# Splitting the turned scores around the key projection in a six-layer local-attention kernel

## The chip, the cores and the metric

The kernel runs on one core of one Trainium2 chip. The metric is the device time of one execution in microseconds (us), and lower is better. A run's time is that of its slowest core, which is here the only one. The engines are called PE (TensorE: MATMUL, with its weight loads LDWEIGHTS, PEld), DVE (VectorE), ACT (ScalarE), POOL (GpSimd) and SP (SyncE, which only starts DMAs here).

## The reference

Input is x of 4 sequences x 512 tokens x 128 features. Stage one is a causal 16-head attention of head size 8 with a linear position bias. Then six layers follow, each a local attention (16 heads of 64, windows of 32 tokens with the window before) and a gated feed-forward part. What matters here is the local attention:

```
x = attn_layer(shift_tokens(x), Wqkv[i], ...) + x        # i = 0..5
x = ffn_layer(shift_tokens(x), ln_g[i], ..., W2[i], b2[i]) + x

attn_layer:  q, k, v = split(x @ Wqkv)                   # 128 -> 3 x 1024
             q, k = l2norm(q) * q_scale, l2norm(k) * k_scale
             q = q*cos*scale + rotate_half(q)*sin*scale  # k with 1/scale
             sim = einsum(q, k of own and previous window) * 8, masked
             out = softmax(sim) @ v @ Wo
ffn_layer:   hg = layernorm(x) @ W1 + b1;  a, gate = split(hg)
             return a * gelu(gate) @ W2 + b2             # 128 -> 2 x 341 -> 128
```

All of it is in 32-bit accuracy: a projection that has to be accurate is made of three products of split halves (high x high, high x low, low x high).

## The kernel before, in words

Each engine has its own program, written out by hand in the block functions, and semaphores tie them together. No scheduler moves anything: the order of the calls is the order on the engine.

**Stage one** (`scores_by_query`, `scores_by_key`, `attend_global`) runs over 16 groups of four heads. In front of two projections of every group PE makes `extra` products into a bank that is overwritten afterwards; the table `EXTRA` holds their number for (group, query or key). They change no result.

**The layers** are 24 bodies, one for a sequence and a layer (6 x 4). Bodies 0 and 1 and the last one are written out; bodies 2 to 22 are one hardware loop. A body has four groups of four heads, and in group n the kernel attends for group n while it projects and rotates group n + 1. For PE a group is, in order: `max_scores(n)` (scores in 16 bits, whose maxima by row steady the softmax), the query projection of n + 1 (two times three 512-column products, one for each half x), one value tile or one feed-forward tile, the first half (x = 0) of the key projection, `turn_max(n)` (the maxima turned by four products with an identity matrix), the second half of the key projection, `turned_scores(n)` (the same scores in 32 bits with keys on the partitions: masks, then 64 small products over four chunks c, then the turned maxima added as a row), `norm2` for queries and keys (sums of squares over a head), and three phases of `attend`, with value tiles, output projection (`out_proj`) and feed-forward products (`up`, `down`, `mean`, `var`) in between.

**The other engines.** ACT squares each projection (L1216), copies value tiles out (L1234), copies the turned maxima into a row (L1241), makes the exponentials (L1248) and the inverse norms (L1222, L1225). DVE takes the maxima in two halves (L1516), multiplies each projection by the cosine and sine tables (L1497, L1498) and writes the finished queries and keys (`final`, L1506). POOL adds the squares (L515), adds the cosine and sine parts (`rotate`, L519 and L520) and, once a body in group 2, splits the next input into a high and a low part (`shifted_input`, L527 to L530).

**PSUM** has eight banks, `ring[i]` being banks 2i and 2i + 1. Queries are projected into 4 and 5, keys into 6 and 7. `max_scores` uses 6, 7, 2 and 3, `turned_scores` 0 to 3, the turned maxima bank 3, and the tile between the projections bank 0. `pe.wait_ge(semaphore, count)` lines guard each reuse.

One product of 32-bit operands is two LDWEIGHTS and two MATMUL rows in the trace; one of the split or of 16-bit operands is one of each. So the 64 small products of `turned_scores` (L893) are 128 MATMUL and 128 LDWEIGHTS.

## Time and profile before

| | us |
|---|---|
| median of 3 runs | 2203.42 |
| lowest, highest | 2201.93, 2210.86 |
| the profiled execution's own time | 2195.48 |
| its span in the trace | 2193.7 |
| the layers' part, about | 340 to 2160 |

The profiled execution is 7.94 us shorter than the median of the runs. The span is the time from the first to the last instruction; the 1.8 us around it are start and end. Busy time counts when an engine had at least one instruction under way; PE's instructions overlap, so the mean of one says less than the distance between two starts. The granted clock of PE was 0.964 of full speed on average, and it is either full (2.4 GHz) or half (1.2 GHz) at any one time. "issue" as a releaser is time in which an engine stood idle though nothing that the profile shows kept it waiting.

### The profile page before, as it was taken

What the parts mean: (1) busy time and instruction counts of PE and PEld (TensorE: products, weight loads), DVE (VectorE), ACT (ScalarE), POOL (GpSimd) and SP (SyncE); (2) the same over time, 40 slices, a digit from 0 to 9 for tenths busy, and PEclk for the clock granted to TensorE, in tenths of its full rate; (3) what the DMA queues carried; (4) which work ended last, traced back from release to release, by engine and by line L of the source; (5) the groups of instructions that cost most, each with busy time, mean ns of one, the idle gap of its engine ahead of it and who ended that gap; (6) DMA issues with size and microseconds to landing.
All of it is one profiled execution on the core that took longest, in us unless ns stands there. A gap on an engine that the chain in (4) does not pass through costs nothing.

```text
span 2193.7 us, 106276 instructions
## 1 busy us (share of the span) xinstructions
PE 1962.0 (89%) x48492; PEld 1321.4 (60%) x48492; DVE 1362.1 (62%) x1447; ACT 1202.3 (55%) x1736; POOL 1102.1 (50%) x1089
## 2 busy tenths in 40 slices
PE   2999986989999999999999999999899999999986
PEld 1444445656666666666566666656666666666663
DVE  4445555676666667666766666676667667666762
ACT  1435555455566555655565665557555556655552
POOL 5223315554675445755546754548545458435440
PEclk9859998999999999999999999999999999999998
DMA  4000000000010000000000100001000001000000
GB/s 131 6 1 2 2 2 12 8 8 5 22 29 18 3 11 16 25 25 9 12 3 23 30 18 3 11 16 31 19 8 12 3 23 29 18 3 12 4 3 20
DMA packets 46922, 34.96 MB, mean 16 GB/s; under 512 B 12804, under 2 KB 43138, under 8 KB 46338
## 3 DMA queue, kind: packets, MB, share of 16 engines
q1 hardware_dynamic: 46466, 27.84, 4.8%
q8 instruction: 414, 6.78, 1.3%
q14 instruction: 42, 0.34, 0.1%
HBM read 20.49 MB, written 1.05 MB: 10 GB/s over the span
## 4 chain that ended last, share of the span: by engine, by line
PE 69%; issue 7%; POOL 4%; DVE 2%; ACT 1%; DVEq 0%; POOLq 0%
PE ring L617 10%; PE ring L934 10%; PE ring L843 7%; PE ring L619 7%; PE ring L618 7%; PE ring L944 7%; PE ring L893 6%; PE ring L975 2%; PE ring L869 2%; PE ring L886 2%; PE ring L862 2%; POOL by_cos L519 2%; POOL by_cos L520 1%; PE ring L952 1%; PE ring L878 1%
## 5 line engine op out<-in xcount | busy, mean ns | idle before, releaser
L515 POOL TENSOR_TENSOR sq_sum<-sq 128x512 f32<-128x512 f32 x192 | 246.3, 1283 | 634.4 <-ACT sq L1216 606.1
L1506 DVE SCALAR_TENSOR_TENSOR fin<-r_norm,by_cos 128x1024 f32<-128x1024 f32 x192 | 275.9, 1437 | 345.4 <-ACT r_norm L1225 281.5
L1216 ACT ACTIVATE sq<-ring 128x1024 f32<-128x1024 f32 x192 | 196.9, 1026 | 308.6 <-PE ring L619 307.2
L1497 DVE TENSOR_TENSOR by_cos<-ring,tabs 128x1024 f32<-128x1024 f32 x192 | 234.3, 1220 | 82.9 <-ACT sq L1216 81.9
L934 PE MATMUL ring<-probs_t,v_sb 64*32 64x96 f32 (+1 forms) x12288 | 280.8, 249 | 4.5 <-issue 2.9
L520 POOL TENSOR_TENSOR by_cos<-by_cos,by_sin 128x512 f32<-128x512 f32 x192 | 276.0, 1437 | 0.0
L934 PEld LDWEIGHTS ring<-probs_t,v_sb 64*32 64x32 f32 x12288 | 214.6, 107 | 93.3 <-issue 87.3
L617 PE MATMUL ring<-parts_sb,w_hi 128*128 128x512 f32 (+1 forms) x528 | 247.5, 469 | 22.2 <-issue 7.0
L519 POOL TENSOR_TENSOR by_cos<-by_cos,by_sin 128x512 f32<-128x512 f32 x192 | 265.9, 1385 | 0.0
L1248 ACT ACTIVATE probs_t<-ring 128x768 f32<-128x768 f32 x192 | 145.1, 808 | 218.1 <-PE ring L900 218.1
L893 PE MATMUL ring<-fin 32*64 32x96 f32 x12288 | 183.9, 253 | 80.3 <-issue 80.3
L1498 DVE TENSOR_TENSOR by_sin<-ring,tabs 128x1024 f32<-128x1024 f32 x192 | 233.0, 1214 | 0.0
L893 PEld LDWEIGHTS ring<-fin 32*64 32x64 f32 x12288 | 172.2, 131 | 90.0 <-issue 89.2
L843 PE MATMUL ring<-sq_sum,wide_sb 128*128 128x128 f32 (+1 forms) x672 | 218.2, 446 | 2.6 <-DVE by_sin L1498 2.6
L619 PE MATMUL ring<-parts_sb,w_lo 128*128 128x512 f32 (+1 forms) x528 | 212.0, 401 | 0.0
L618 PE MATMUL ring<-parts_sb,w_hi 128*128 128x512 f32 (+1 forms) x528 | 211.4, 400 | 0.0
L1516 DVE TENSOR_REDUCE neg_max<-ring 128x8 bf16<-128x768 f32 x192 | 175.3, 958 | 47.1 <-PE ring L869 46.8
L934 PE MATMUL ring<-probs_t,ones 64*32 64x96 f32 (+1 forms) x6144 | 186.5, 251 | 11.2 <-issue 8.7
L1222 ACT ACTIVATE r_norm<-ring,wide_sb 128x512 f32<-128x512 f32 x192 | 131.7, 686 | 104.0 <-PE ring L843 103.8
L934 PEld LDWEIGHTS ring<-probs_t,ones 64*32 64x32 f32 x6144 | 139.0, 108 | 75.5 <-issue 73.4
L944 PE MATMUL ring<-o_feat,wo_sb 128*128 128x128 f32 (+1 forms) x936 | 182.9, 346 | 0.9 <-DVE state L1529 0.9
L1424 DVE TENSOR_REDUCE row_max<-ring 128x2 f32<-128x256 f32 (+3 forms) x128 | 103.7, 823 | 124.4 <-PE ring L680 123.7
(168 smaller groups left out, 3456.2 us busy)
## 6 DMA issues: line engine op xcount, KB each, us to landing
w_raw<-in_L_ffn_Wqkv SPq DMA_DIRECT2D x48, 192.0 KB, 2.8
wo_sb<-in_L_ffn_Wo SPq DMA_DIRECT2D x48, 64.0 KB, 2.0
x_in<-state SPq DMA_DIRECT2D x24, 128.0 KB, 2.6
x_in<-state SPq DMA_DIRECT2D x24, 127.8 KB, 3.5
w_raw<-in_L_ffn_W SPq DMA_DIRECT2D x6, 341.0 KB, 4.1
rot_sb<-in_rotary SPq DMA_DIRECT2D x1, 1024.0 KB
out<-x_tok SPq DMA_DIRECT2D x16, 64.0 KB, 1.6
by_cos<-in_masks SPq DMA_DIRECT2D x1, 896.0 KB
```

The source lines that it names most:

```text
L515: pool.tensor_tensor(sq_sum[:, i, :], sq[:, i, 0, :], sq[:, i, 1, :], ALU.add).then_inc(s_ss[i], 1)
L519: pool.tensor_tensor(rotated[:, i, 0, :], by_cos[:, i, 0, :], by_sin[:, i, 1, :], ALU.add)
L520: pool.tensor_tensor(rotated[:, i, 1, :], by_cos[:, i, 1, :], by_sin[:, i, 0, :], ALU.add).then_inc(s_rot[i], 1)
L617: pe.matmul(dst, lh, rh, start=True, stop=False)
L618: pe.matmul(dst, lh, rl, start=False, stop=False)
L619: return pe.matmul(dst, ll, rh, start=False, stop=True)
L843: mm = pe.matmul(bank[4 + 2 * i][:, own], head_ones, sq_sum[:, i, own], start=True, stop=True)
L893: pe.matmul(bank[r][half(e), c * REACH:(c + 1) * REACH], k_fin[head_rows(r), x, WINDOW + at:WINDOW + at + HALF_P], q_fin[head_rows(r), x, ...
L934: mm = pe.matmul(dst, w, p, start=start, stop=True, skip_group_check=True)
L944: mm = pe.matmul(bank[(5, 7)[half_]][:, own], wo_sb[:, a, :], o_feat[:, a, own], start=(a % GPB == 0 and k == 0), stop=(a % GPB == GPB - 1 ...
L1497: dve.tensor_tensor(by_cos[:, i, :, :], ring[2 + i][:], tabs[:, i, 0, :, :], ALU.mult)
L1506: dve.scalar_tensor_tensor(out=dst, in0=r_norm[:, i, :].unsqueeze(1).to_broadcast([P, 2, TOK]), scalar=NORM_CAP, in1=rotated[:, i, :, :], ...
```

## The change

1. **`turned_scores` is cut in two.** It no longer waits for the turned maxima at its start. Chunks 0 and 1 (with the masks) come directly after `turn_max`; then both halves of the key projection; then chunks 2 and 3; and the turned maxima are added at the end by `take_maxima`. `turn_max` itself moves ahead of the first half of the key projection. The wait for the copied maxima stands between the two halves of the key projection, because bank 7 is now both.
2. **Other banks.** The turned maxima go to bank 7 instead of 3, and the tile between the projections to bank 6 instead of 0. The tile now waits for the first half of the maxima (`s_mx`, 2n + 1), and the key projection for the tile to be copied out (`keys_banks_free`).
3. **The input split moves from POOL to DVE**, between the key tables and `final` of the queries in group 2. POOL's order inside a group changes too: sum of the queries' squares, half of the queries' rotation, sum of the keys' squares, and then the other three quarters of the rotations.
4. **No column pieces.** In group 0 `norm2` and the second `out_proj` were made in four pieces of 128 columns; now each is one product of 512 columns, as in the other groups.
5. **Stage one.** The one entry of `EXTRA` above 1 goes from 25 to 77, and products of such an entry become 64 columns wide instead of 512.

```diff
-EXTRA = {(2, 0): 25, (2, 1): 1, (3, 0): 1, ...
+EXTRA = {(2, 0): 77, (2, 1): 1, (3, 0): 1, ...
...
+            def rotary(n):
+                sum_squares(n, 0)
+                rotate(n, 0, 0)
+                sum_squares(n, 1)
+                rotate(n, 0, 1)
+                rotate(n, 1, 0)
+                rotate(n, 1, 1)
...
             def extra(count):
+                width = TOK if count == 1 else HALF_P
                 for _ in range(count):
-                    pe.matmul(TURN_BANK[:], eye16, mask_sb[:, 0:TOK], start=True, stop=True)
+                    pe.matmul(TURN_BANK[:, 0:width], eye16, mask_sb[:, 0:width], start=True, stop=True)
...
-            def turned_banks_free(n, g, grp, age):
-                if not (isinstance(n, int) and n == 0):
-                    pe.wait_ge(s_nrm, n)
+            def keys_banks_free(n, g, grp, age, nxt):
                 if grp == 0:
                     pe.wait_ge(s_ve, V_HALF * (2 * g + 1) + 1)
                 if grp == 1:
                     pe.wait_ge(s_ve, V_HALF * (2 * g + 1) + 3)
                 if grp == 2 and age > 1:
                     pe.wait_ge(f_he, NF * g - NF)
+                if grp == 3 and nxt:
+                    pe.wait_ge(s_ve, V_HALF * (2 * g + 2) + 2)
...
-            def turned_scores(n):
-                pe.wait_ge(s_nm, n + 1)
+            def turned_scores(n, chunks):
+                if chunks[0] == 0:
...
-                for c in range(CHUNKS):
+                for c in chunks:
...
+            def take_maxima(n):
+                pe.wait_ge(s_nm, n + 1)
...
-                    if not (isinstance(n, int) and n == 0):
-                        pe.wait_ge(s_nrm, n)
+                    pe.wait_ge(s_mx, 2 * n + 1)
                     if grp == 0:
-                        value_tile(g, 1, 0, 0)
+                        value_tile(g, 1, 0, 6)
...
+                    turn_max(n)
+                    if not (isinstance(n, int) and n == 0):
+                        pe.wait_ge(s_nrm, n)
+                    turned_scores(n, (0, 1))
                     if nxt:
-                        pe.wait_ge(s_mx, 2 * n + 1)
+                        keys_banks_free(n, g, grp, age, nxt)
                         project(n + 1, gn, grp_n, 1, parts=(0,))
-                    turn_max(n)
-                    if nxt:
+                        pe.wait_ge(s_nm, n + 1)
                         project(n + 1, gn, grp_n, 1, parts=(1,))
-                    turned_banks_free(n, g, grp, age)
-                    if grp == 3 and nxt:
-                        pe.wait_ge(s_ve, V_HALF * (2 * g + 2) + 2)
-                    turned_scores(n)
+                    turned_scores(n, (2, 3))
+                    take_maxima(n)
...
-                        norm2(n + 1, 0, 4 if grp == 0 else 1)
+                        norm2(n + 1, 0)
...
+            def shifted_input(g):
+                dve.wait_ge(s_xin, 32 * (g + 1))
+                dve.tensor_copy(xs_hi, x_in[:]).then_inc(s_xhi, 1)
+                dve.wait_ge(s_xhi, g + 1)
+                dve.tensor_tensor(xs_lo, x_in[:], xs_hi.bitcast(F32), ALU.subtract).then_inc(s_xs, 1)
...
                         times_tables(n + 1, l, 1)
+                    if grp == 2 and not last:
+                        dve.wait_ge(s_p[1], GPB * (g + 1))
+                        dve.wait_ge(s_v, V_HALF * (2 * g + 2))
+                        shifted_input(g + 1)
```

How the instructions move on PE in the loop, group 1. Names: `parts_sb,w_hi` or `w_lo` are projections and tiles, `neg_max` the maxima, `fin` the finished queries and keys, `neg_row` the copied maxima. Before, from the end of the value tile:

```order
L617 MATMUL ring<-parts_sb,w_hi 128x512
L618 MATMUL ring<-parts_sb,w_hi 128x512
L619 MATMUL ring<-parts_sb,w_lo 128x512
L876 REGISTER_ALU
L878 MATMUL ring<-mask_sb,neg_max 128x128 x4
L617 MATMUL ring<-parts_sb,w_hi 128x512
L618 MATMUL ring<-parts_sb,w_hi 128x512
L619 MATMUL ring<-parts_sb,w_lo 128x512
L824 REGISTER_ALU
L886 MATMUL ring<-mask_sb 64x384 x16
L893 MATMUL ring<-fin 64x96 x64
L900 MATMUL ring<-neg_row,ones 64x384 x8
```

And the same place in the changed kernel:

```order
L866 MATMUL ring<-mask_sb,neg_max 128x128 x4
L874 MATMUL ring<-mask_sb 64x384 x16
L881 MATMUL ring<-fin 64x96 x32
L813 REGISTER_ALU
L607 MATMUL ring<-parts_sb,w_hi 128x512
L608 MATMUL ring<-parts_sb,w_hi 128x512
L609 MATMUL ring<-parts_sb,w_lo 128x512
L607 MATMUL ring<-parts_sb,w_hi 128x512
L608 MATMUL ring<-parts_sb,w_hi 128x512
L609 MATMUL ring<-parts_sb,w_lo 128x512
L881 MATMUL ring<-fin 64x96 x32
L891 MATMUL ring<-neg_row,ones 64x384 x8
```

The block of 64 small products has become two of 32, with all six products of the key projection between them, and the turned maxima stand directly ahead of the first block.

On DVE in group 2 the changed kernel has, between the four table products and the finished queries and keys:

```order
L1503 TENSOR_REDUCE neg_max<-ring 128x2x4 x2
L1484 TENSOR_TENSOR by_cos<-ring,tabs 128x1024
L1485 TENSOR_TENSOR by_sin<-ring,tabs 128x1024
L1484 TENSOR_TENSOR by_cos<-ring,tabs 128x1024
L1485 TENSOR_TENSOR by_sin<-ring,tabs 128x1024
L1509 CAST parts_sb<-x_in 128x512
L1511 TENSOR_TENSOR parts_sb<-x_in,parts_sb 128x512
L1493 SCALAR_TENSOR_TENSOR fin<-r_norm,by_cos 128x2x512 x2
```

L1509 and L1511 are the input split, which on POOL stood between the two rotations of the same group.

## Rows read from the trace of the kernel before

**Rows 1.** Page, head and parts 1 and 3: instructions, busy time, queue of instructions (packets, MB)

```profile
span 2193.7 us, 106276 instructions
...
PE 1962.0 (89%) x48492; PEld 1321.4 (60%) x48492; DVE 1362.1 (62%) x1447; ACT 1202.3 (55%) x1736; POOL 1102.1 (50%) x1089
...
q8 instruction: 414, 6.78, 1.3%
```

**Rows 2.** Windows: us; busy (count) PE, PEld, DVE, ACT, POOL; clock; DMA share, GB/s

```profile
104.30:158.90 54.60, 54.16 (x461) 25.79 (x459) 19.82 (x37) 21.49 (x34) 13.52 (x11) 0.50 0.00 1
158.90:216.90 58.00, 52.18 (x806) 28.90 (x807) 34.09 (x68) 33.34 (x59) 17.81 (x14) 1.00 0.01 2
340.00:2160.00 1820.00, 1673.87 (x45045) 1170.47 (x45044) 1191.23 (x1092) 1041.40 (x1468) 996.88 (x966) 0.98 0.05 14
```

**Rows 3.** PE's waits, whole trace: who for, us in total, times, longest us

```profile
PE ring L893 <- issue: 80.3, 46, 2.2
...
PE ring L934 <- issue: 11.7, 15, 1.8
PE ring L862 <- issue: 9.2, 12, 1.4
```

**Rows 4.** Timeline, a group 1: start, us, engine, line, count [idle before]

```profile
1044.67 0.40 PE L617 MATMUL ring<-parts_sb,w_hi 128*128 128x512 f32 x1
...
1045.09 0.59 ACT L1234 ACTIVATE v_sb<-ring 128x512 f32<-128x512 f32 x1
...
1045.37 0.40 PE L878 MATMUL ring<-mask_sb,neg_max 128*128 128x128 bf16 x4
1045.58 0.48 PE L617 MATMUL ring<-parts_sb,w_hi 128*128 128x512 f32 x1
...
1046.55 0.53 PE L886 MATMUL ring<-mask_sb 32*64 32x384 bf16 x16
1046.87 1.44 PE L893 MATMUL ring<-fin 32*64 32x96 f32 x100
1050.24 0.49 PE L893 MATMUL ring<-fin 32*64 32x96 f32 x23 [1.92 <-issue]
```

**Rows 5.** Windows: between two gaps; ahead of a gap; a dense stretch without one

```profile
1029.14:1048.32 19.18, 19.06 (x502) 15.77 (x503) 9.27 (x10) 13.64 (x18) 7.21 (x9) 1.00 0.01 3
1045.50:1048.32 2.82, 2.78 (x124) 2.14 (x122) 2.79 (x3) 1.81 (x3) 1.73 (x2) 1.00 0.03 6
1064.64:1068.20 3.56, 3.56 (x140) 2.10 (x123) 3.15 (x3) 2.00 (x3) 3.00 (x3) 1.00 0.02 5
```

**Rows 6.** Timeline, group 2 of the same body, which has no gap

```profile
1060.20 1.83 DVE L1516 TENSOR_REDUCE neg_max<-ring 128x8 bf16<-128x768 f32 x2 [0.65 <-PE ring L869]
...
1062.90 0.40 PE L878 MATMUL ring<-mask_sb,neg_max 128*128 128x128 bf16 x4
...
1063.66 0.40 PE L619 MATMUL ring<-parts_sb,w_lo 128*128 128x512 f32 x1
...
1064.10 1.03 ACT L1216 ACTIVATE sq<-ring 128x1024 f32<-128x1024 f32 x1 [0.16 <-PE ring L619]
1064.40 1.71 PE L893 MATMUL ring<-fin 32*64 32x96 f32 x124
...
1066.59 1.21 DVE L1498 TENSOR_TENSOR by_sin<-ring,tabs 128x1024 f32<-128x1024 f32 x1
1069.08 1.13 PE L843 MATMUL ring<-sq_sum,wide_sb 128*128 128x512 f32 x2
```

**Rows 7.** Timeline of that group: the input split on POOL, and DVE's next instruction

```profile
1069.72 1.28 POOL L530 TENSOR_TENSOR parts_sb<-x_in,parts_sb 128x512 fp32r<-128x512 f32 x1
1069.78 2.30 DVE L1506 SCALAR_TENSOR_TENSOR fin<-r_norm,by_cos 128x1024 f32<-128x1024 f32 x1 [1.99 <-ACT r_norm L1225]
```

**Rows 8.** Timeline: `norm2` in pieces; the 25 extra products

```profile
1033.28 1.06 PE L843 MATMUL ring<-sq_sum,wide_sb 128*128 128x128 f32 x8
59.35 7.52 PE L653 MATMUL ring<-mask_sb 128*128 128x512 bf16 x25
```

More of the change, by code:

```diff
@@ L558, in body @@
                     if not (last and grp == GPB - 1):
-                        for i in range(2):
-                            sum_squares(n + 1, i)
-                        rotate(n + 1, 0)
-                        if grp == 2 and not last:
-                            pool.wait_ge(s_p[1], GPB * (g + 1))
-                            pool.wait_ge(s_v, V_HALF * (2 * g + 2))
-                            shifted_input(g + 1)
-                        rotate(n + 1, 1)
+                        rotary(n + 1)
                         if grp == 0:
@@ L590, in _ @@
                 split_group(g, 1)
-            shifted_input(0)
-            for i in range(2):
-                sum_squares(0, i)
-            for i in range(2):
-                rotate(0, i)
+            rotary(0)
             def layer(l, first=False, last=False):
@@ L836, in project, with norm2 @@
                     mm.then_inc(s_p[i], 1)
-            def norm2(n, i, pieces=1):
+            def norm2(n, i):
                 pe.wait_ge(s_tab[i], n + 1)
                 pe.wait_ge(s_ss[i], n + 1)
-                for k in range(pieces):
-                    own = slice(k * TOK // pieces, (k + 1) * TOK // pieces)
-                    mm = pe.matmul(bank[4 + 2 * i][:, own], head_ones, sq_sum[:, i, own], start=True, stop=True)
-                mm.then_inc(s_n2[i], 1)
+                pe.matmul(bank[4 + 2 * i], head_ones, sq_sum[:, i, :], start=True, stop=True).then_inc(s_n2[i], 1)
             def value_tile(g, half_, c, b):
@@ L877, in turn_max @@
                 for c in range(CHUNKS):
[L878 removed]
+                    mm = pe.matmul(bank[7][:, c * P:(c + 1) * P], neg_max[:, c, :], eye16, start=True, stop=True)
                 mm.then_inc(s_tm, 1)
[L881 to L888 removed]
+            def turned_scores(n, chunks):
+                if chunks[0] == 0:
+                    for b in range(2):
+                        for e in range(2):
+                            for r in range(GROUP):
+                                pe.matmul(bank[r][half(e), 0:NEAR], eye_half[head_rows(r), b, :],
+                                          near_mask[head_rows(r), b, :], start=(b == 0), stop=False)
+                for c in chunks:
                     for x in range(2):
@@ L941, in out_proj @@
                 for a in (GPB * half_ + 2 * part, GPB * half_ + 2 * part + 1):
-                    for k in range(pieces):
-                        own = slice(k * TOK // pieces, (k + 1) * TOK // pieces)
-                        mm = pe.matmul(bank[(5, 7)[half_]][:, own], wo_sb[:, a, :], o_feat[:, a, own],
-                                       start=(a % GPB == 0 and k == 0), stop=(a % GPB == GPB - 1),
-                                       skip_group_check=pieces > 1)
+                    mm = pe.matmul(bank[(5, 7)[half_]], wo_sb[:, a, :], o_feat[:, a, :], start=(a % GPB == 0), stop=(a % GPB == GPB - 1))
                 if part == 1:
@@ L1240, in max_row @@
                     act.wait_ge(s_st, n)
-                act.activation(neg_row[:, 0:TOK], bank[3], ACT.Copy).then_inc(s_nm, 1)
+                act.activation(neg_row[:, 0:TOK], bank[7], ACT.Copy).then_inc(s_nm, 1)
             def exps(n):
```

45 lines of the change are left out of this document (17 added, 28 removed).

## The prediction, made before the changed kernel was run

> **What bounds the kernel now.** I read the totals first [rows 1]: PE is busy for 89% of the span and no other engine for more than 62%, so PE's own stream sets the time unless someone makes it wait. Then the windows, to see where [rows 2]: the layers take 1820 of 2193.7 us, PE is busy for 1673.87 us of them at a clock of 0.98, so about 146 us are idle. Then PE's waits [rows 3]. What stands out is not a wait for another engine. It is "issue", idle time with no semaphore behind it: 80.3 us in 46 gaps ahead of L893, the small products of the turned scores, and 9.2 us in 12 gaps ahead of L862, the first line of a group. The timeline shows one such gap [rows 4]: 100 of the 128 MATMULs run without a break, then PE, and its weight loads with it, stop for 1.92 us in the middle of a run of equal instructions whose operands are all there. In the next group the same code runs 124 of them in one go [rows 6]. So the gap does not belong to the operation but to its place.
>
> That place can be counted. A whole window from the end of the gap in group 0 to the start of the gap in group 1 holds 502 MATMULs and 503 weight loads [rows 5]; with some 18 waits and register instructions between, that is about 1023. The instructions arrive by DMA in packets of 6.78 MB / 414 = 16.4 KB, and all packets together give some 64 bytes for each of the 106,276 instructions [rows 1], so about 256 in a packet. The two gaps lie four packets apart. I conclude that PE ran out of instructions: the next packet was not there yet. Ahead of the gap 246 instructions had gone by in 2.82 us; with the gap it took 4.74 us until the next came. In group 2 a dense stretch of 263 instructions that took 3.56 us had no gap [rows 5]. So a packet that is used up in about 3.5 us costs nothing or little, one used up in 2.8 us costs some 1.75 us (80.3 / 46).
>
> The Trainium skill ("Runtime: NRT & Kernel Launch", section "Instruction fetch mechanics") says that instructions are refilled in 16 KiB blocks of 256 and that crossing a block is "mostly hidden". The size agrees with the trace's 16.4 KB; "mostly hidden" does not, with 80.3 us of gaps. If that sentence held, the gaps would have another cause, and the change would save none of them; this is the first rival below. The page also says that a taken branch out of the current window forces a fetch; 12 gaps at L862, which also stands first behind the loop's branch, fit that.
>
> **The split of the turned scores.** No matmul goes away, so PE's busy time in these lines stays. What changes is how dense they stand. Before, 32 + 256 + 16 rows of masks, scores and maxima follow each other. Now the densest 256 rows of a group begin at the turned maxima: 4 products in 0.21 us (1062.90 to the next start, as 1045.37 to 1045.58 [rows 4]), masks 0.32 us (1046.55 to 1046.87), 64 MATMULs at 12 ns (124 in 1.71 us less the 0.24 us of the last) 0.77 us, a hand-over of 0.2, six projection products at 0.23 us (1044.67 to 1045.37 is three) 1.4 us, a hand-over of 0.1, and 38 more MATMULs 0.46 us: 3.46 us. That is the length of the dense stretch that had no gap. Ends for what stays at such a place: 0, and 4.74 - 3.46 = 1.3 us. I take 0.4 us, near the row without a gap, at three places in a body (groups 0, 1 and 3). The 80.3 us at L893, less 24 x 3 x 0.4 = 29, give **-51 us**, with ends of -80 and, at 1.3 us each, +13.
>
> The gap at L862 sits at the loop's edge, where the packets are cut differently after the change: 0, ends -9 and +9.
>
> **The wait for the copied maxima.** Three projection products from 1045.58, at 0.23 us and 0.1 more for the first, would have let the next start at 1046.37; L886 started at 1046.55 [rows 4]. I credit half of the 0.18 us, since a hand-over to small products costs something in any case. The masks no longer wait for the copy: 95 x 0.1 = **-9 us**, ends 0 and -19. Ahead of the second half of the keys the copy has 64 MATMULs and three products, some 2.3 us, for its 0.9 us.
>
> **What is now waited for.** The maxima are needed 0.70 us earlier, at 1044.67 instead of 1045.37 in rows 4. In group 2 they end at 1060.20 + 1.83 = 1062.03, and PE comes there at 1062.90 - 0.70 = 1062.20: 0.17 us of room [rows 6]. The tile's bank has to be copied out before the keys: ready at 1045.68, wanted at 1044.67 + 0.21 + 0.32 + 0.77 + 0.2 = 1046.17: 0.5 us of room [rows 4]. The real risk is the key chain. The last key product starts 2.8 us behind the new start of the turned maxima (1.5 + 1.25), so at 1065.0 in rows 6 instead of 1063.66, 1.3 us later, while the end of the turned scores stays where it is. Square 0.44 + 1.03, tables 2.35: by_sin ends at 1068.85, and norm2 of the keys, which overwrites the bank that by_sin reads, wants to start at 1069.08. The room falls from 1.28 to 0.2 us in group 2; in group 0 a feed-forward tile adds 0.7 us to it. Behind that norm2 the second and third attend phases would queue, and ACT behind them. I take **+8 us** in all for short waits (under 0.1 us a group); ends 0 and +30 (0.3 us a group).
>
> **The input split** leaves POOL, where the larger of its two instructions takes 1.28 us, for DVE, which sat idle for 1.99 us just there, waiting for ACT [rows 7]. DVE's two instructions are not in the trace of before in this form; bounds by the nearest rows are 0 and, with both as long as POOL's, 2.6 us together; I take 1.4. It fits into the idle 1.99 us; at 2.6 the finish of the queries begins 0.6 us late, and that of the keys gains from POOL's rotation of the keys, which no longer stands behind the split. Ahead of the first body it lies open: -1. In the loop 0, ends -5 and +14 (0.6 us in 23 bodies).
>
> **No pieces.** Eight MATMULs of 128 columns took 1.06 us [rows 8], two of 512 took 1.13 [rows 6]: the same within 0.1. With 48 norm2 and 46 output projections: -3, ends -9 and +7. The 72 fewer rows in group 0 thin its packets a little, which is in the 0.4 above.
>
> **Stage one.** The 25 products took 7.52 us [rows 8], where the clock rose in between. 77 products of 64 columns, each with a full weight load: 53 ns at full clock by L878's four in 0.21 us, twice that at half: 4.1 to 8.2 us. I take 6: **-1.5 us**. What the clock does afterwards I can't tell. At half clock PE made 461 MATMULs in 54.6 us, at full 806 in 58.0 [rows 2], so this stretch cost 54.6 - 461/13.9 = 21 us. Without it up to 21 us would be saved; half clock from 60 to 94 us too would cost, at the same rate, 34 x 21/54.6 = 13.
>
> **Sum.** -51 - 9 + 8 - 1 - 3 - 1.5 = -57.5 us, on the profiled execution's 2195.5 us: 2138. Its time lay 7.9 us below the median of the runs, most likely by the clock in stage one, so for the median **2203.4 - 57.5 = 2146 us**.
>
> **The rivals.**
> The gaps stay or only move: with the same 256 rows in a packet they turn up in other dense stretches, the attend phases for instance, or they have another cause. For it: the work and the number of packets are the same, and the attend phases at L934 are made of the same small products. Against it: these already stand apart by wide products, and show 11.7 us in 15 gaps where L893 shows 80.3 in 46 [rows 3]. Then only -9 + 8 - 5.5 is left: 2197, no change. Chance 0.09.
> All gaps go and nothing replaces them: -80 - 9 (L862) - 9 - 5.5 + 2 = -101.5: 2102. Chance 0.12.
> Slower: the key chain is late. Place: norm2 of the keys, behind by_sin. It decides as soon as by_sin ends over 0.2 us later than worked out, for instance because POOL's quarter rotation, now at the same time, slows DVE (its finish of the queries in rows 7, beside POOL's work, took 2.30 us, nearly twice by_sin's 1.21 for as many elements). If two table products take half as long again, 1.2 us, PE waits 1.0 us in each of 95 groups: +95 against -65 for the rest: 2233. Against it: by_cos and by_sin ran beside POOL's sums in rows 6 without loss. Chance 0.07.
> Stage one runs colder: the narrow products leave the clock at half in the stretch from 60 to 94 us as well: +13 us on the forecast: 2159. Chance 0.10.
>
> **How the numbers follow.** Forecast 0.62. A measurement of this kernel tells changes over 0.5% (11 us) from none. Faster gathers the forecast, the total loss of gaps and the cold stage: 0.84. Same is the first rival: 0.09. Slower is the third: 0.07. The forecast's own range, from 0.1 to 0.8 us at each of the 72 places, is 2124 to 2175. The whole range reaches down to 2106, nearly the total loss of the gaps, and up to 2197, where they are all back; the slower case and half of the first rival lie above it, some of the second below, together under 0.2.
>
> **What would show it.** Right: L893 (two shorter groups of x64 a group of heads) shows issue gaps of under 0.6 us or none, PE's issue time at the turned scores falls from 80 to under 35 us, a body takes 2 to 3 us less. Wrong: gaps of over 1 us ahead of any line; PE waiting ahead of norm2 with DVE's by_sin as the releaser; PE ahead of the turned maxima waiting for L1516's successor; a clock of 0.5 for more than 60 us of stage one.

## The result, and the profile after

The changed kernel took 2103.46 us (median of 4 runs, 2081.72 to 2150.82), the kernel before beside it 2207.14 us (2201.93 to 2214.99). The ratio is 0.9527, 95% interval [0.9458, 0.9597]: faster by 4.7%, about 100 us. The forecast was 2146 us with a range from 2106 to 2197, so the gain was larger than its low end allowed. The profiled execution took 2092.28 us. Single times of the changed kernel spread over 70 to 84 us with stage one's clock (below); the ratios leave out the slower ones among them.

The page after, its head and parts 1 and 3, and the windows of the layers [answer to rows 1 and 2]:

```profile
span 2089.8 us, 104591 instructions
...
PE 1950.5 (93%) x47704; PEld 1233.0 (59%) x47704; DVE 1427.0 (68%) x1495; ACT 1190.5 (57%) x1736; POOL 1087.3 (52%) x1017
...
q8 instruction: 405, 6.64, 1.4%
```

```profile
104.30:158.90 54.60, 49.87 (x720) 26.64 (x712) 30.53 (x61) 30.53 (x55) 17.79 (x14) 0.94 0.01 2
158.90:216.90 58.00, 55.70 (x578) 27.61 (x578) 24.42 (x45) 25.25 (x39) 15.24 (x12) 0.65 0.01 2
340.00:2070.00 1730.00, 1670.76 (x44231) 1083.06 (x44231) 1261.20 (x1146) 1037.07 (x1477) 985.57 (x900) 0.99 0.06 15
```

PE's busy time in the layers is what it was (1670.76 us, before 1673.87 [rows 2]); the idle time went from 146 to 59 us. PE's waits say which [rows 3]:

```profile
PE ring L857 <- issue: 11.2, 21, 0.9
PE ring L850 <- DVE fin L1493: 10.5, 10, 1.4
...
PE ring L607 <- issue: 6.4, 23, 2.9
PE ring L850 <- issue: 6.1, 14, 0.7
PE ring L607 <- DVE parts_sb L1511: 5.6, 1, 5.6
...
PE ring L925 <- issue: 4.0, 7, 0.7
PE ring L866 <- DVE neg_max L1503: 3.3, 3, 2.3
...
PE ring L832 <- DVE by_sin L1485: 2.0, 1, 2.0
...
PE ring L881 <- issue: 0.7, 3, 0.3
```

L881 is the turned scores' line (L893 before): 80.3 us in 46 gaps have become 0.7 in 3. L925 is L934 of before: 11.7 to 4.0. L850 is L862: 9.2 to 6.1. Grown is L857, the 16-bit scores: from 1.4 us in 3 gaps (L869 before) to 11.2 in 21, of half a microsecond each. The timeline of a group 1 shows the new order without a stop [rows 4]:

```profile
1005.31 0.40 PE L866 MATMUL ring<-mask_sb,neg_max 128*128 128x128 bf16 x4
1005.64 0.53 PE L874 MATMUL ring<-mask_sb 32*64 32x384 bf16 x16
1005.99 1.00 PE L881 MATMUL ring<-fin 32*64 32x96 f32 x64
...
1006.92 0.50 PE L607 MATMUL ring<-parts_sb,w_hi 128*128 128x512 f32 x1
1007.25 0.39 PE L608 MATMUL ring<-parts_sb,w_hi 128*128 128x512 f32 x1
...
1008.50 0.98 PE L881 MATMUL ring<-fin 32*64 32x96 f32 x60
...
1009.79 1.12 PE L939 MATMUL ring<-x_sh,wide_sb 128*128 128x512 f32 x2
```

**A cleaner measure than the total.** The loop's branch has a row of its own, with its first and last start; between them lie 20 bodies. Before, then after:

```profile
L1076 PEldq COMPARE_BRANCH  x21: 83/3695/4798, 560.4 to 2075.8; - x21
```

```profile
L1063 PEldq COMPARE_BRANCH  x21: 83/3676/3921, 550.9 to 1980.4; - x21
```

A body took 1515.4 / 20 = 75.77 us and takes 1429.5 / 20 = 71.48. Ahead of the first branch 9.5 us were won (stage one and bodies 0 and 1), in the 20 bodies 85.9, behind the last branch 8.5: together the 103.9 us by which the spans differ.

**Where the 4.29 us of a body come from**, tallied from the matmul rows of the 20 bodies, idle pieces above 0.15 us: gaps fell from 5.25 to 1.59 us, -3.7. The half clock makes another -0.8: before, 51.2 us of the 20 bodies ran at half clock, in 15 stretches; after, 6.8 us in 2. Bodies without any half clock took 74.69 us before (7 of them) and 71.20 after (18), so it cost 1.08 and 0.28 us a body on average. In 14 of the 15 cases such a stretch began 0.3 to 1.7 us behind the end of a gap of over 1 us; 29 more gaps of over 1 us had none behind them (first lines of a group left out). Windows of before, ahead of, behind and in one of them:

```profile
799.00:802.40 3.40, 1.84 (x118) 1.60 (x117) 2.91 (x3) 1.02 (x1) 2.19 (x2) 1.00 0.02 5
802.40:804.00 1.60, 1.49 (x39) 1.13 (x40) 0.12 (x1) 0.71 (x1) 1.60 (x3) 1.00 0.00 0
804.00:807.40 3.40, 3.40 (x74) 2.93 (x73) 0.05 (x1) 2.21 (x4) 2.41 (x2) 0.50 0.02 5
```

and its timeline:

```profile
802.51 0.49 PE L893 MATMUL ring<-fin 32*64 32x96 f32 x22 [1.66 <-issue]
...
803.98 1.86 PE L843 MATMUL ring<-sq_sum,wide_sb 128*128 128x128 f32 x8
```

After the 1.66 us gap the clock fell to 1.2 GHz at 804.0, and the eight products that take 1.06 us in rows 8 took 1.86.

### The profile page after: what moved, and what is told of

Read it like the earlier page. It is cut to its first block, busy times and chain, and to the rows that moved or that the text cites. A ratio compares the mean times of both kernels' runs of the same rounds, so it can differ in the third digit from the quotient of the medians.

```text
span 2089.8 us, 104591 instructions
## 1 busy us (share of the span) xinstructions
PE 1950.5 (93%) x47704; PEld 1233.0 (59%) x47704; DVE 1427.0 (68%) x1495; ACT 1190.5 (57%) x1736; POOL 1087.3 (52%) x1017
## 4 chain that ended last, share of the span: by engine, by line
PE 87%; DVE 4%; issue 3%; POOL 2%; ACT 1%; DMA 1%; SPq 0%; DVEq 0%; ACTq 0%; POOLq 0%
PE ring L607 12%; PE ring L925 11%; PE ring L832 8%; PE ring L881 8%; PE ring L609 8%; PE ring L608 8%; PE ring L933 7%; PE ring L962 3%; PE ring L857 3%; PE ring L711 3%; PE ring L874 2%; PE ring L850 2%; PE ring L654 1%; PE ring L691 1%; PE ring L939 1%
## 5 line engine op out<-in xcount | busy, mean ns | idle before, releaser
L519 POOL TENSOR_TENSOR by_cos<-by_cos,by_sin 128x512 f32<-128x512 f32 x384 | 568.5, 1502 | 119.3 <-DVE by_sin L1485 119.3
L1493 DVE SCALAR_TENSOR_TENSOR fin<-r_norm,by_cos 128x1024 f32<-128x1024 f32 x192 | 284.6, 1491 | 105.5 <-ACT r_norm L1212 59.7
L925 PEld LDWEIGHTS ring<-probs_t,v_sb 64*32 64x32 f32 x12288 | 211.1, 106 | 121.1 <-issue 120.4
L925 PE MATMUL ring<-probs_t,v_sb 64*32 64x96 f32 (+1 forms) x12288 | 272.6, 246 | 3.9 <-issue 2.2
L607 PE MATMUL ring<-parts_sb,w_hi 128*128 128x512 f32 (+1 forms) x528 | 247.9, 469 | 19.9 <-issue 6.4
L832 PE MATMUL ring<-sq_sum,wide_sb 128*128 128x512 f32 x384 | 206.1, 619 | 2.6 <-DVE by_sin L1485 2.0
L881 PEld LDWEIGHTS ring<-fin 32*64 32x64 f32 x12288 | 175.6, 130 | 40.0 <-issue 36.0
L881 PE MATMUL ring<-fin 32*64 32x96 f32 x12288 | 198.0, 251 | 0.7 <-issue 0.7
L925 PE MATMUL ring<-probs_t,ones 64*32 64x96 f32 (+1 forms) x6144 | 179.8, 246 | 4.1 <-ACT probs_t L1235 2.3
L933 PE MATMUL ring<-o_feat,wo_sb 128*128 128x512 f32 x384 | 179.0, 599 | 0.9 <-DVE state L1522 0.9
L925 PEld LDWEIGHTS ring<-probs_t,ones 64*32 64x32 f32 x6144 | 133.3, 105 | 76.6 <-issue 76.6
L1221 ACT ACTIVATE v_sb<-ring 128x512 f32<-128x512 f32 x192 | 113.2, 590 | 60.7 <-PE ring L609 60.2
```

The lines of the kernel that those rows point to most:

```text
L519: rot = pool.tensor_tensor(rotated[:, i, x, :], by_cos[:, i, x, :], by_sin[:, i, 1 - x, :], ALU.add)
L607: pe.matmul(dst, lh, rh, start=True, stop=False)
L832: pe.matmul(bank[4 + 2 * i], head_ones, sq_sum[:, i, :], start=True, stop=True).then_inc(s_n2[i], 1)
L881: pe.matmul(bank[r][half(e), c * REACH:(c + 1) * REACH], k_fin[head_rows(r), x, WINDOW + at:WINDOW + at + HALF_P], q_fin[head_rows(r), x, ...
L925: mm = pe.matmul(dst, w, p, start=start, stop=True, skip_group_check=True)
L933: mm = pe.matmul(bank[(5, 7)[half_]], wo_sb[:, a, :], o_feat[:, a, :], start=(a % GPB == 0), stop=(a % GPB == GPB - 1))
```

## The experiments

Several runs change only the placement: waits already met are put at PE's start, so that all later instructions move against the packets of 256 in which they are fetched. In the compiled programs the first packet of a loop body ends at instruction 187 of it in the kernel before and at 186 in the changed one, the next 256 later, and so on. The gaps in the traces stand at these places. Ratios are to the kernel before on the same chip; "half" is the half clock inside the 20 bodies.

| run | median us | ratio, 95% interval | body us | half us |
|---|---|---|---|---|
| before_shift96 | 2252.55 | 1.0290 [1.0198, 1.0382] | 77.58 | 109 |
| before_shift16 | 2240.21 | 1.0229 [1.0141, 1.0318] | 78.63 | 85 |
| before_split_dve | 2202.69 | 1.0049 [0.9956, 1.0142] | 75.87 | 61 |
| after_shift128 | 2177.34 | 0.9953 [0.9903, 1.0004] | 75.30 | 75 |
| after_joined | 2199.86 | 0.9963 [0.9895, 1.0031] | 75.59 | 17 |
| joined_bank0 | 2128.43 | 0.9681 [0.9589, 0.9773] | 72.58 | 3 |
| after_pieces | 2183.12 | 0.9874 [0.9754, 0.9995] | 75.22 | 72 |
| after_pieces_placed | 2120.23 | 0.9635 [0.9528, 0.9742] | 71.53 | 7 |
| after_poolsplit | 2174.49 | 0.9917 [0.9876, 0.9959] | 74.62 | 31 |
| after_poolorder | 2140.65 | 0.9779 [0.9691, 0.9868] | 73.11 | 21 |
| after_extra25 | 2101.14 | 0.9628 [0.9558, 0.9698] | 71.48 | 14 |
| after_shift224 | 2089.89 | 0.9464 [0.9385, 0.9542] | 71.53 | 14 |
| after_again | 2089.52 | 0.9421 [0.9364, 0.9478] | 71.42 | 10 |
| warm2 | 2086.27 | 0.9462 [0.9416, 0.9508] | 71.36 | 10 |
| warm3 | 2098.62 | 0.9531 [0.9486, 0.9576] | 71.68 | 0 |

### Are the gaps the supply of instructions? (placement alone)

The trace holds the start and the landing of every packet on the instruction queue. These are windows of the kernel before around the gap of [rows 4]; the last two columns are the DMA share and GB/s:

```profile
1044.44:1047.60 3.16, 3.13 (x90) 2.31 (x93) 2.36 (x2) 2.87 (x4) 1.29 (x1) 1.00 0.00 0
1047.60:1047.70 0.10, 0.10 (x33) 0.10 (x17) 0.09 (x1) 0.00 (x0) 0.04 (x1) 1.00 0.79 162
1048.32:1050.24 1.92, 0.00 (x1) 0.00 (x1) 1.65 (x2) 0.00 (x0) 1.92 (x3) 1.00 0.00 0
```

The one packet started at 1047.65 and landed at 1048.92. PE had stopped at 1048.32 and went on at 1050.24, 1.3 us behind the landing. In the loop of the kernel before there are 43 issue gaps of over 1 us that don't stand at the first line of a group, and each of them ends 1.2 to 1.5 us behind such a landing. In all kernels of this document together it is 257 gaps, all 1.2 to 1.6 us behind a landing, on a queue that brings a packet in 5.3 us on average (414 in 2193.7 us). PE did wait for its instructions.

But the packet ahead of this gap was not used up in 2.8 us. Its 256 instructions began at 1044.44, so they lasted 3.9 us. The packet of group 2 that began at 1064.60 lasted 3.6 us, a little less, and had no gap behind it. What differs is when the next fetch starts: 3.2 us behind the packet's first instruction in group 1, 0.9 us in group 2 (at 1065.45). Over the 20 bodies it is 3.3 and 3.4 us on average in groups 0 and 1, where each body stops, and 0.9 us in group 2, where none does; in the changed kernel it is 0.7 us at the same two places. In groups 0 and 1 of the kernel before the fetch started 1.0 to 1.7 us behind the first mask.

```diff
-            pe.wait_ge(s_const, 16 * CONST_LOADS)
+            for _ in range(257):   # after_shift128; 193 in before_shift96, 33 in before_shift16
+                pe.wait_ge(s_const, 16 * CONST_LOADS)
```

Two such waits make one instruction.

> The changed kernel with 128 more instructions at the very start of PE's program (waits that are long satisfied, while PE waits for the first input anyway), so that the same loop lies 128 instructions later. Supply theory: packets of 256 are cut at other places; one cut falls 58 instructions behind the top of the loop, in the 16-bit scores of group 0, and a gap of 1 to 3 us appears there in every body: 73 to 75 us a body, 2125 to 2170 us in all. Rival (what counts is the order of the instructions or the waits, not their place in memory): no change, 71.5 us a body.

> The kernel before with 96 more instructions at the start of PE's program, as in after_shift128. Supply theory: the gaps behind 100 and 101 of the 128 turned-score MATMULs of groups 0 and 1 vanish from there; the cuts now fall 91 behind the loop's top (in the 16-bit scores of group 0) and at about 2395 (in the turned scores of group 2, behind roughly 100 MATMULs), and gaps of 1.5 to 3 us show there; a body stays at 75 to 78 us, the whole at 2195 to 2245. Rival (the gap belongs to groups 0 and 1, by a wait or a bank): gaps stay in groups 0 and 1.

> The kernel before, with 16 more waits that are already met at its start on TensorE, so that every later instruction stands 16 places further in the packets of 256; nothing in the loop is changed. In the kernel before the packet ends fall at places 187, 443, 699 and so on of the loop's body, and the turned scores of groups 1 and 2 stop behind 123 and 23 matmuls of it; here they fall at 171, 427, 683, which puts the first into single-cost projection work and leaves the gaps of groups 0 and 1 the most cover. Supply theory (the turned scores waited because a packet was used up faster than the next came): idle time of PE ended by 'issue' in the turned scores falls from 80 us to under 25, the body of the loop from 75.8 to 74.0-74.8 us, and the kernel comes out at 0.98 to 0.99 of the kernel before, by placement alone. What then remains between it and the changed kernel's 71.5 us is the worth of the change itself. Rival (the gaps belong to the order of the work, for instance to bursts of too many matmuls without a wait): 16 places of shift change nothing, body 75.5-76.0, ratio 1.00.

With 128 instructions ahead, the first packet of a body ends at 58, within the 16-bit scores, and the changed kernel loses 3.8 us a body. That is a little more than expected (75.30 us a body, 2177.34 in all); the expectation had no half clock in it. This gap is of another kind: behind the loop's branch PE is through the 58 instructions in under a microsecond. Its timeline:

```profile
621.38 0.28 PE L858 MATMUL ring<-fin 32*64 32x96 bf16 x11
623.80 0.68 PE L858 MATMUL ring<-fin 32*64 32x96 bf16 x53 [2.14 <-issue]
```

```profile
PE ring L858 <- issue: 43.3, 21, 2.6
...
PE ring L851 <- issue: 19.1, 15, 1.6
```

In the kernel before, 96 instructions moved the gaps out of groups 0 and 1 of the turned scores into group 2 (47.0 us at L894, behind 99 matmuls) and the 16-bit scores of group 0:

```profile
PE ring L894 <- issue: 47.0, 25, 2.3
...
PE ring L870 <- issue: 42.8, 22, 2.4
```

Here too the whole came out above its range (2252.55 us for 2195 to 2245), with the body within it. With 16 instructions the gap moved by eight matmuls, from behind 101 to behind 93:

```profile
636.60 1.37 PE L894 MATMUL ring<-fin 32*64 32x96 f32 x93
639.90 0.62 PE L894 MATMUL ring<-fin 32*64 32x96 f32 x34 [1.94 <-issue]
```

So the place of a gap is the packet's end. But my expectation for these 16 was wrong (as was its count: the gaps of before stand behind about 100 matmuls, in groups 0 and 1): the gaps did not shrink (81.0 us) and the body became 2.9 us longer, of which the half clock explains part. Why they did not shrink is in the packets again. With 16 wide-product rows more in it the packet lasted 5.4 us instead of 4.0, and PE stopped behind it for 1.8 to 1.9 us all the same, since the next fetch started only 4.8 us behind the packet's first instruction, again 1.1 us behind the first mask. So for these gaps the pace at which a packet is used up does not decide, but when the next fetch starts. What holds it back in front of the turned scores is not isolated by any run.

### What the order of the turned scores is worth

after_joined (the scores in one piece behind the key projection):

```diff
-                    turned_scores(n, (0, 1))
                     if nxt:
                         keys_banks_free(n, g, grp, age, nxt)
                         project(n + 1, gn, grp_n, 1, parts=(0,))
...
+                    turned_scores(n, (0, 1))
                     turned_scores(n, (2, 3))
```

> The changed kernel with the turned scores in one piece again, behind both halves of the key projection; banks, waits ahead of the masks, input split, norm2 and stage one stay as changed. Supply theory (PE runs out of instructions where 256 of them pass in under about 3.5 us): gaps of over 1 us come back in the turned scores in at least one group, the loop body takes 73 to 75 us instead of 71.5, the whole 2125 to 2170 us. Rival (the gain is that the scores no longer wait for the copied maxima, and the other banks): the projection half behind that wait keeps it, so at most 0.2 us a group comes back, 20 us, and no issue gap of over 1 us.

It lost nearly the whole gain (75.59 us a body, above both expectations), in two ways at once: there was a gap in group 1 again, now directly behind the scores, and the key projection waited for the tile's bank, which had nothing in front of it any more. Group 0 had no gap.

```profile
PE ring L607 <- ACT v_sb L1221: 47.9, 71, 0.9
...
PE ring L891 <- issue: 29.0, 22, 1.7
PE ring L607 <- DVE gates L1553: 17.8, 22, 0.8
```

joined_bank0 removes the second: as after_joined, but the tile goes to bank 0 again and the banks' wait stands behind the key projection.

```diff
-                        value_tile(g, 1, 0, 6)
+                        value_tile(g, 1, 0, 0)
...
                         project(n + 1, gn, grp_n, 1, parts=(1,))
+                    keys_banks_free(n, g, grp, age, nxt)
                     turned_scores(n, (0, 1))
```

> The changed kernel with the turned scores in one piece behind the key projection (as in after_joined), but with the tile between the projections in bank 0 again, so that the keys don't wait for its copy. That takes the v_sb waits out of after_joined (48 us ahead of L607) and leaves what density alone does. Supply theory: one or two places with a gap of 1 to 2 us a body in groups 0 and 1, body 73 to 74.5 us, whole 2130 to 2165 us. Rival (the joined kernel lost only by the bank waits): body 71.5 us, whole within 15 us of 2100.

It keeps all but 1.1 us of a body, which lies between the two expectations. Its waits, and the scores of a group 0:

```profile
PE ring L607 <- ACT neg_row L1227: 30.5, 71, 0.7
PE ring L939 <- issue: 14.6, 21, 1.2
...
PE ring L881 <- issue: 4.0, 5, 1.1
```

```profile
1036.94 1.71 PE L881 MATMUL ring<-fin 32*64 32x96 f32 x124
```

This run says most about the change, because the packets end where they did. In group 0 the end falls behind matmul 100 to 102 of the 128 in the kernel before, in after_joined, here and in the changed kernel. The kernel before stops there in 20 of 20 bodies, for 1.8 us. Here the block is in one piece too and passes in 15 of 20 bodies (0.8 us in the other five), and in after_joined in all 20. The next fetch started 1.0 and 0.8 us behind the packet's first instruction on average, not 3.3. So most of the 80.3 us went without the scores being cut: in one piece, 4.0 us are left in them and 14.6 directly behind them, where the packet of group 1 ends (L939). What the cut saves beside this kernel lies in these 18 us of gaps and in the waits for the copied maxima at L607 (30.5 us): 1.1 us a body in all. The rest of the gaps went with something else that these kernels share: the turned maxima ahead of the key projection and in bank 7, or the wait for their copy no longer directly ahead of the masks. No run takes one of these alone. Parts 3 to 5 were each put back alone (below), and next to no gaps came back in the turned scores (1.6 us in all at most); part 3 alone left those of the kernel before as they were (80.8 us in before_split_dve). Of after_joined's loss the bank's waits (65.7 us) were the larger part, and the gap (29.0 us) the smaller.

### The column pieces

```diff
-                        norm2(n + 1, 0)
+                        norm2(n + 1, 0, 4 if grp == 0 else 1)
...
-                            out_proj(f, 1, 1)
+                            out_proj(f, 1, 1, 4)
```

after_pieces brings the pieces back (96 instructions ahead of the loop, 72 in a body); after_pieces_placed is the same with 160 more at the start, so that the first packet of a body ends at 186 again.

> The changed kernel with norm2 and the second output projection of group 0 in four column pieces again. That puts 96 more instructions ahead of the loop and 72 more into its group 0. Supply theory: a cut falls 90 behind the loop's top, in the 16-bit scores of group 0, with a gap of 1.5 to 2.7 us in each body: body 73.5 to 75 us, whole 2140 to 2180. Rival (pieces cost what their instructions cost, under 0.2 us a body): whole within 15 us of 2103.

> As after_pieces, with 160 more instructions at the start of PE's program, so that the first cut of the loop falls 186 behind its top, as in the changed kernel. Supply theory: the gap of after_pieces is gone although the kernel only grew: body 71.3 to 72 us, whole 2095 to 2120 us. Rival (pieces are dear by themselves): like after_pieces.

75.22 against 71.53 us a body: the pieces cost nothing themselves (71.48 without them). Their instructions, by moving the packets, cost 3.7 us, as a gap of up to 2.4 us in the 16-bit scores of group 0 and its half clock. That is slightly more than expected, in the body and in the whole.

### The input split and POOL's order

after_poolsplit puts the input split back on POOL, between the halves of the rotation, and both sums of squares first; after_poolorder only the sums; before_split_dve is the kernel before with DVE's split and the new order of POOL.

```diff
                 sum_squares(n, 0)
-                rotate(n, 0, 0)
                 sum_squares(n, 1)
+                rotate(n, 0, 0)
                 rotate(n, 0, 1)
```

> The changed kernel with the input split on POOL again, between the two rotations of group 2, and POOL's old order of sums and rotations. PE's program is unchanged, cuts included. If this part carries any of the gain (POOL's rotation, or DVE and POOL at the same time), the body is 0.3 us or more slower and PE waits for fin ahead of the 16-bit scores; I expect 71.5 us a body and a whole within 15 us of 2103, beside 1 to 2 us for a later first projection.

> The changed kernel with GpSimd's sums of squares both ahead of its rotations, as before, in place of one behind the other in turn; the input's split stays on VectorE. It tells which half of the third part carries the 3.1 us of a body that the changed kernel lost when both were taken back. If it is the order on GpSimd (the sum of squares of the second half comes later or earlier for the key's norm): body 73.5-74.8 us and PE's waits at the norm's matmul (ended by VectorE's fin) at 40 us or more. If it is the split alone, which in GpSimd's queue stood between two rotations once in four groups: body 71.4-71.9, ratio to the kernel before as the changed kernel's, 0.95 to 0.965. I hold the second the likelier, 0.6 to 0.4, since GpSimd's 2.3 us of split stands in a queue that is busy for over half of the time; but the wait had 49 counts, more than one per group 3.

> The kernel before with only the third part of the change: the input's split into two parts is done by VectorE, and GpSimd's sums and rotations are interleaved as in the changed kernel. TensorE's instructions and their places are those of the kernel before. Theory (TensorE is held by its supply of instructions there, so what GpSimd delivers earlier is not used): body 75.4-76.0 us, ratio 0.995 to 1.005, the gaps in the turned scores as before at 75-85 us. Rival (this part is a gain of its own, as the 3.1 us of a body that the changed kernel lost without it suggest): body 73 or less, ratio under 0.97.

In the kernel before, this part is worth nothing. In the changed one it carries 3.1 us a body, where I had expected none: 1.6 by POOL's order and another 1.5 by the split, so neither of the two answers that I had set up for after_poolorder. The first product of a group waits for the finished queries and keys. after_poolsplit (L867 is L850 of the changed kernel):

```profile
PE ring L867 <- DVE fin L1510: 64.3, 49, 2.9
...
PE ring L867 <- DVE gates L1570: 22.4, 22, 1.4
```

and after_poolorder:

```profile
PE ring L850 <- DVE fin L1493: 36.0, 28, 2.7
PE ring L850 <- DVE gates L1553: 22.3, 22, 1.4
```

against 10.5 us in the changed kernel, which waits for no gates there. With the gaps gone PE reaches the group's end sooner, and the chain through POOL and DVE becomes what it waits for.

### Stage one and its clock

after_extra25 has the 25 wide products of before, the loop placed as in the changed kernel. after_shift224 moves the packets' ends from 186 to 218. warm2 and warm3 have two and three wide products in the 27 places that had one.

```diff
-(2, 1): 1, (3, 0): 1, ...
+(2, 1): 2, (3, 0): 2, ...
-                width = TOK if count == 1 else HALF_P
+                width = TOK if count == 2 else HALF_P
```

> The changed kernel with stage one's 25 wide products instead of 77 narrow ones, and 104 instructions more at the start so that the loop lies where it lay. If the narrow products are what makes the runs spread (2082 to 2151 us) by PE's clock in stage one: a spread of under 20 us and a median of 2095 to 2115. If not: the same spread, and a median within 15 us of 2103. The loop body stays at 71.5 us in both.

> The changed kernel with 224 more waits already met at its start on TensorE, so that the packet ends of the loop's body fall at 218, 474 and so on in place of 186, 442: 32 places further. Supply theory: no packet is used up faster than the next comes at either place, so nothing in the middle changes; the small gap behind 29 matmuls of the 16-bit scores in one group of four (11 us in all) moves into the projection and goes, body 71.0-71.5 us, ratio to the kernel before 0.945 to 0.96. Rival (any shift of the start by a hundred or more instructions costs some 4 us a body, as 128 did, whatever place it lands on): body 75, ratio 0.99.

> The changed kernel once more, beside the two below on the same chip, for the spread of its own stage one. Ratio to the kernel before 0.945 to 0.96; body of the loop 71.2-71.7 us; time under the half clock before the loop anywhere from 60 to 240 us, and the single time follows it with about a third of a microsecond for each.

> The changed kernel with two products of 512 columns in place of one at each of the 27 places of stage one that had one (27 more, 5.7 us of work by 0.21 us each, whose results nobody reads), and TensorE's packets placed two instructions from the changed kernel's. Stage one runs for 60 to 240 us under the half clock, and one count of half clock costs about 0.34 us. If the clock falls in stage one because TensorE has too little to do in it, the additional products keep it up: half clock before the loop under 60 us, the median 10 to 30 us below the changed kernel's of this call, spread narrower. Rival (where the clock falls is not set by these few products): half clock as before, the median 0 to 8 us above the changed kernel's.

> As the one ahead, with three products of 512 columns at each of the 27 places (54 more, 11 us by 0.21 us each). If more work keeps the clock up: half clock before the loop under 40 us, the median within 5 us of the one with two, or lower. Rival: 5 to 14 us above the changed kernel's median.

The 77 narrow products took 4.24 us where 25 wide ones took 7.52 [rows 8], and nothing else is seen of them: with either the first branch of the loop stands at 551 us and a body takes 71.48, and the six runs with the wide ones spread over 35 us, between the two expectations. 32 instructions of shift changed nothing; the small gap, which I had expected to go, went from behind 29 to behind 45 matmuls of the same scores (9.3 us). With the additional products the clock stayed up: the mean granted clock of single runs lay at 0.976 to 0.989 in warm2 and 0.981 to 0.986 in warm3, and at 0.933 to 0.983 in the changed kernel beside them. Ahead of the loop the half clock lasted 44 us in warm2's profile and 58 in warm3's (expected: under 40), and 61 to 266 us in the others' (99 in the changed kernel's first). Windows 100 to 350, after_again and then warm2:

```profile
100.00:350.00 250.00, 229.38 (x2876) 118.05 (x2868) 116.96 (x224) 121.65 (x203) 61.02 (x48) 0.79 0.01 2
```

```profile
100.00:350.00 250.00, 214.85 (x2941) 114.85 (x2949) 125.28 (x236) 131.63 (x218) 69.49 (x54) 0.91 0.02 4
```

The single times lay between 2077.46 and 2091.50 us for warm2, 2096.79 and 2107.83 for warm3, and 2070.28 and 2153.91 for the changed kernel beside them. warm2's median is 3 us lower, where I had expected 10 to 30; that isn't told apart from none, and its ratio is not better. warm3's is 12 us above warm2's, as its rival had it; its trace has 26.6 us of issue gaps at L607 for 6.9 in warm2's, one of 0.95 us in each body. warm2's best run is 7 us worse, about the price of 27 products, and its worst of 6 runs is 62 us better than the changed kernel's worst of 7. Where steady times count it is the version to keep.

## Why the prediction was wrong

That PE ran out of instructions was right. The rule for when it does was not, and with it the main size. The second rival, that all gaps go and nothing replaces them, named 2102 us and got a chance of 0.12. That it comes within 2 us of the measured 2103 is in part luck: it has -9 for L862 and -9 for the copied maxima, and no clock. By the prediction's terms:

| term | forecast us | measured us |
|---|---|---|
| gaps at the turned scores | -51 | -79.6 (80.3 to 0.7) |
| half clock in the loop | none | -17 (0.80 x 21 bodies) |
| gaps at L934 | none | -7.7 (11.7 to 4.0) |
| gap at L862 | 0 | -3.1, and +9.8 at L857 (1.4 to 11.2) |
| wait for the copied maxima | -9 | about +17, below |
| new waits | +8 | +1 (turned maxima for neg_max, 2.3 to 3.3) |
| input split ahead of the first body | -1 | -1.0 (6.6 to 5.6) |
| input split in the loop | 0 | 0 on the kernel before; 3.1 a body as part of the whole |
| pieces | -3 | about -1 (0.05 a body) |
| the 25 and 77 products | -1.5 | -3.3 |

The measured column adds up to -85 of the 103.2 us by which the profiled executions differ. The rest of a group, with the gaps taken out and at full clock, is shorter by 0.2 us a body, another -4; some -14 are assigned to nothing.

**The step that failed** is the rule "a packet that is used up in about 3.5 us costs nothing or little, one used up in 2.8 us costs some 1.75 us", and the size taken from it, "I take 0.4 us, near the row without a gap, at three places in a body". The 2.82 us of [rows 5] hold 246 of the packet's 256 instructions. The ten ahead of them, most of them of wide products, take another 1.1 us, so the packet lasted 3.9 us, longer than the one without a gap. The rule then kept 29 us of gaps where 0.7 were left. What the runs show in its place is the start of the next fetch, 3.3 us behind the packet's first instruction before and 0.7 us after. It also follows that the split of the scores, to which the prediction gave the -51 us, is not what removed most of the gaps (joined_bank0). Within the prediction's own rule, too, the nearest row, 3.56 us without a gap, said 0. I had worked out 3.46 us from durations at full overlap; the timeline after shows 1005.31 to 1008.50, 3.19 us, for the turned maxima, masks, 64 matmuls and six products, where I had summed 3.0. With the 0.46 us of the 38 more matmuls I estimate 3.65 us.

**The step that was missing** is the clock. I took the loop's 0.98 as given. It went with the gaps: 14 of the 15 stretches at 1.2 GHz in the loop stand right behind one of 1 to 2 us. The window's 0.98 [rows 2] was a row that I had read and not asked about.

**A term with the wrong sign.** The time from the query projection to the end of the turned scores, gaps taken out, rose from 25.49 to 26.31 us in bodies at full clock: 0.2 us a group, +17 in 21 bodies, instead of -9. The extra changes between small and wide products cost it: from the turned maxima to the masks 0.33 us where I had 0.21, and 0.33 instead of 0.23 for the first product behind the scores.

**The first rival** (the gaps move elsewhere) is the other kernel one gets at another placement: after_shift128 came out at 0.9953. So a large part of the 4.7% rests on where the packets happen to end, and I had weighed this rival only by what stands in the dense stretches, not by a packet that ends right behind the loop's branch. **The third** (key chain late at `norm2`) did not occur: L832 waited once for by_sin, 2.0 us. A chain did lie close behind, though another: the finished queries and keys at the group's first product, which part 3 keeps ahead. **The fourth** (stage one colder) can't be told from the spread that stage one has anyway.

The Trainium skill ("Runtime: NRT & Kernel Launch", section "Instruction fetch mechanics") calls the crossing of a block "mostly hidden". A body crosses some 15 blocks; the runs agree for most of these crossings, and disagree for the one to three at which PE stopped, with up to 3.8 us a body.

## What to carry to other kernels

Where PE stops in a run of equal small products with "issue" as the releaser, count the instructions from gap to gap, and look when the instruction queue's packets landed. If the distances are multiples of 256 and each gap ends behind a landing, try another order of the work and the waits around that place, and another placement with idle instructions at the start, before judging any other edit. Count a packet from its first instruction: what seems the dense part of it may be less than the whole. An edit that adds or removes instructions ahead of a loop may win or lose 4 us a body for that reason alone: compare it with the placement restored. And ask of every gap which clock follows it, and which chain is late once it is gone.

## What the runs showed of the hardware that I had not expected

- PE went on 1.2 to 1.6 us behind the landing of a packet of instructions in all 257 issue gaps of over 1 us away from a group's first line. The fetch of the next packet started 0.7 us behind the first instruction of the one before at the two places of the changed kernel and 0.9 us in group 2 of the kernel before, but 3.3 to 4.8 us behind it where the kernel before and its shifted versions stop in the turned scores; why stays open.
- Half clock can follow short idleness. In after_shift128 each of 19 half-clock stretches in the loop stood at a gap of 1.8 to 2.6 us in the 16-bit scores; bodies there took 75.30 us on average, the one without a stretch 73.0.
- 16 instructions at the start made the kernel before 2.3% slower though its gaps in the turned scores kept their size (80.3 and 81.0 us). 1.3 us of the 2.9 a body is left if only bodies at full clock are compared (75.99, two bodies, against 74.69), and 11.4 us at L844 and 12.3 us at L619 are new, where other packets end now. Why the clock fell so much more often, 25 times for 15, stays open.
- 27 more products of 512 columns, whose results nobody reads, took the spread of single times from 84 us (7 runs) to 14 (6 runs) and left the median where it was.
